# A four-layer graph network on one core: the flag load of SP moved ahead of its store waits, and sixteen identity transposes at the start of TensorE

## The reference

```python
h = jnp.maximum(_layernorm(x, axis=-1), 0.0)
x = x + _L0_gnn_ref(h, adj, L0_gnn_W, L0_gnn_a)     # GAT: Wh, e = leaky(s1 + s2), masked softmax, attention @ Wh
h = jnp.maximum(_layernorm(x, axis=-1), 0.0)
x = x + _L1_gnn_ref(h, adj, a0, a1, a2, a3)         # four edge kinds, scores (h*a_r) @ h.T picked by adj, softmax, @ h
h = jnp.maximum(_layernorm(x, axis=-1), 0.0)
x = x + _L2_gnn_ref(h, None, adj, weight, bias)     # RGCN: sum over kinds of mask @ h @ weight_r, + bias
h = jnp.maximum(_layernorm(x, axis=-1), 0.0)
x = x + _L3_gnn_ref(h, adj, L3_gnn_W, L3_gnn_a)     # GAT again, then elu
```

## Time and profile before

| what | value |
|---|---|
| median of three executions | 287.89 us (287.56 to 288.56) |
| the profiled execution's own time | 288.05 us |
| its span, first to last instruction | 285.8 us |
| instructions | 8113 |
| TensorE, VectorE, ScalarE, GpSimd busy | 96%, 88%, 89%, 82% |
| HBM traffic | 13.05 MB read, 4.19 MB written, 60 GB/s over the span |

### The profile page before, as it was taken

How to read it: one execution, slowest core, us unless ns; L and a number is a source line. 1 busy time by engine, 2 the same in 40 slices (tenths; PEclk the granted TensorE clock), 3 DMA queues, 4 the chain that set the end, 5 groups by cost and what they waited for, 6 DMA issues and landing times.

```text
span 285.8 us, 8113 instructions
## 1 busy us (share of the span) xinstructions
PE 274.3 (96%) x2252; PEld 257.9 (90%) x2252; DVE 251.9 (88%) x1217; ACT 255.0 (89%) x850; POOL 234.1 (82%) x376
## 2 busy tenths in 40 slices
PE   3999999999999999999999999999999999998991
PEld 2999998888889999999999999888889999998991
DVE  4889999988878887899999999998898888799985
ACT  5998988799998888999999999799999889796994
POOL 4998787777747999999999988887755899999722
PEclk9999999999999999999999999999999999999998
DMA  6946645400000000015333201000000000001213
GB/s 216 319 127 179 177 142 147 167 2 2 0 0 3 0 2 2 3 37 150 98 109 114 73 22 41 18 18 2 1 2 1 3 0 0 3 3 54 76 58 115
DMA packets 15414, 17.79 MB, mean 62 GB/s; under 512 B 2180, under 2 KB 11272, under 8 KB 15368
## 3 DMA queue, kind: packets, MB, share of 16 engines
q1 hardware_dynamic: 15220, 17.18, 19.9%
q10 hardware_dynamic: 148, 0.07, 0.1%
HBM read 13.05 MB, written 4.19 MB: 60 GB/s over the span
## 4 chain that ended last, share of the span: by engine, by line
PE 87%; DVE 8%; ACT 2%; issue 1%; POOL 0%; DVEq 0%; POOLq 0%
PE bank L1001 26%; PE bank L943 10%; PE bank L919 9%; PE bank L948 9%; PE bank L877 7%; PE bank L986 5%; PE bank L956 5%; PE bank L968 5%; PE bank L998 4%; PE bank L903 3%; PE bank L950 2%; DVE pT L699 2%; DVE expy L735 1%; PE bank L922 1%; DVE st L624 1%
## 5 line engine op out<-in xcount | busy, mean ns | idle before, releaser
L367 POOL TENSOR_TENSOR rs<-mv,minus_half 128x2 f32<-128x2 f32 x128 | 89.8, 702 | 35.5 <-DVE mv L635 35.0
L1001 PE MATMUL bank<-val,pT 128*128 128x129 f32 x512 | 74.6, 275 | 0.0
L1001 PEld LDWEIGHTS bank<-val,pT 128*128 128x128 f32 x512 | 67.3, 192 | 0.0
L384 POOL TENSOR_TENSOR h<-h,rs 128x256 f32<-128x256 f32 x93 | 58.2, 626 | 2.3
L699 DVE SCALAR_TENSOR_TENSOR pT<-bank,val,edgesT 128x256 f32<-128x256 f32 x128 | 55.0, 471 | 0.8 <-PE bank L956 0.7
L624 DVE BATCH_NORM_STATS2 st<-x 128x6 f32<-128x128 f32 x192 | 45.2, 276 | 0.0
L527 ACT ACTIVATE val<-bank,val 128x128 f32<-128x128 f32 x128 | 44.3, 437 | 0.1
L635 DVE BATCH_NORM_AGGREGATE mv<-st 128x2 f32<-128x9 f32 x256 | 33.5, 172 | 10.8 <-DVE st L624 1.0
L919 PE MATMUL bank<-w_gat,hT 128*128 128x131 f32 x256 | 40.3, 281 | 0.0
L376 POOL TENSOR_TENSOR h<-x,mv 128x256 f32<-128x256 f32 x64 | 40.1, 626 | 0.0
L877 PE MATMUL bank<-ident,h 128*128 128x128 f32 x192 | 38.0, 280 | 1.4 <-ACT hT L495 1.1
(11 more groups left out here) (87 smaller groups left out, 662.7 us busy)
## 6 DMA issues: line engine op xcount, KB each, us to landing
edges<-in_adj SPq DMA_DIRECT2D x32, 256.0 KB, 2.9
xin<-in_x SPq DMA_DIRECT2D x32, 128.0 KB, 2.6
out_x<-result SPq DMA_DIRECT2D x32, 128.0 KB, 1.7
w_rel<-in_L_gnn_weight SPq DMA_DIRECT2D x1, 256.0 KB, 2.8
w_gat<-in_L_gnn_W ACTq DMA_DIRECT2D x1, 64.0 KB
w_gat<-in_L_gnn_W SPq DMA_DIRECT2D x1, 64.0 KB
a_rel<-in_L_gnn_a SPq DMA_DIRECT2D x4, 0.5 KB, 3.0
bias<-in_L_gnn_bias SPq DMA_DIRECT2D x1, 64.0 KB, 3.3
```

What stands on the lines that cost most here:

```text
L367: pool.tensor_tensor(rs[:, n % WIDE], mv[:, n % WIDE, :, 1], minus_half[:, :], ALU.pow).then_inc(rs_ready, 1)
L384: pool.tensor_tensor(h[:, n % HS, :, 0:D], h[:, n % HS, :, 0:D], rs[:, n % WIDE, :].rearrange("p (t o) -> p t o", o=1).to_broadcast([P, T, ...
L1001: last = pe.matmul(bank_o(n)[:, t], pT[:, n % 4, u, t * P:(t + 1) * P], values[:, u], start=(u == 0 and layer == 1), stop=(u == T - 1), sk ...
```

## The change

SP's program waits for the flag and loads it right after the last store was issued. The eight waits for the stores stand in a function now, which is called first thing inside the general program and once more behind the branch. TensorE gets a function spin, which transposes the identity into bank 7 so many times: eight times ahead of put_wT, four times between put_wT and put_wa, four times behind put_wa. Nothing reads what these transposes write.

```diff
             pipeline([(load_x, SP_LAG, FIRST), (load_edges, SP_LAG, FIRST), (store, SP_LAG + 1, LAST)])
-            for k in range(SLOTS):
-                sp.wait_ge(stored[k], 16 * ROUNDS)
+            def all_stored():
+                for k in range(SLOTS):
+                    sp.wait_ge(stored[k], 16 * ROUNDS)
 
             sp.wait_ge(flag_ready, 1)
             with sp.If(sp.value_load(flag[0:1, 0:1], min_val=0, max_val=P) > 0):
+                all_stored()
                 sp.sem_inc(g_step, 1)
                 sp.sem_inc(g_stored, 16)
...
                 sp.wait_ge(g_stored, 16 * B + 16)
+            all_stored()
...
+            def spin(times):
+                for _ in range(times):
+                    pe.transpose(bank[7][:, 0:P], ident[:, :], ident[:, :])
+
+            spin(8)
             put_wT(0, ps_w)
+            spin(4)
             put_wa(0, ps_w)
+            spin(4)
```

## The result

Four executions of the changed kernel took 290.57 to 291.25 us, median 291.02, against 287.89 before. The ratio is 1.0105, with a 95% interval of 1.0091 to 1.0119: slower by 3.1 us. I had forecast 287.8, with a range of 286.9 to 288.6.

What follows compares the result with a forecast made beforehand. TensorE was taken as the bound, idle only near start and end, with ScalarE equally limiting the start. The profiled 288.05 us, +0.37 at the start and -0.45 at the end, gave 287.97; 0.16 lower on the median, 287.8, range 286.9 to 288.6.

Steps and rivals of the forecast that it cites:

- They write a bank that nothing uses yet, so they cost only TensorE's time and queue place.: Start: the sixteen identity transposes cost only TensorE time, 0.215 us each; first transpose of h 1.05 us late.
- tail: End: the execution's time less the time at which VectorE has written the flag; 4.46 us in the kernel before.
- Rival B: Start: TensorE's clock rises later, following the later real work; 288.3 if moved rigidly, up to 289.4; chance 0.12.
- The gain of 0.45 us at the end: End: SP loads the flag before its store waits, leaving VectorE's drain at 285.1 last; 0.45 us saved.
- 0.37 us late: Start: exponentials and L956 of graph 3 come later, 0.57 from ScalarE less 0.20 won back.
- the gate: Start: L956 of graph 3, near 16.1 us, claimed to be reached by TensorE and ScalarE within 0.1 us.
- The 0.57 of ScalarE: Start: ScalarE's mask moves from 8.61 to 9.18 us, 0.57 late, with ScalarE back to back from there.
- The 0.20 to be won back: Start: ScalarE's 0.25 us wait for TensorE's L903 transposes before 11.44 shrinks by 0.20 with a faster TensorE.
- The rise of the clock near 7.9 us: Start: if identity transposes count as work, TensorE reaches 2.4 GHz near 7.9 us instead of about 11.2.
- Rival A: Start: the transposes leave the clock where it was, rising at 11.2 us; 287.95 on the median; chance 0.20.
- ScalarE as the limit of the start: Start: ScalarE runs back to back from 8.61 us, so time saved on TensorE alone buys nothing.
- rival C: Start: TensorE alone decides when L956 of graph 3 starts, so 1.2 us counts in full; 286.2; chance 0.12.

Runs made afterwards that it cites:

- e9: Kernel before plus sixteen identity transposes in TensorE's general program, which doesn't run: 290.23 us, ratio 1.0071.
- e4: The change with 36 instruction records taken out of TensorE's general program, which doesn't run: 287.61 us, ratio 0.9986.
- e10: The change plus sixteen identity transposes at TensorE's idle end: 287.71 us, ratio 0.9975.
- e14: e9 plus sixteen identity transposes at TensorE's idle end: 287.68 us, ratio 0.9983 to the kernel before.
- e7: The change plus two identity transposes at TensorE's idle end: 291.09 us, ratio 1.0111 to the kernel before.
- e1: SP's part alone, the change without its spin calls: 287.93 us, ratio 1.0008 to the kernel before.
- e5: SP's part plus sixteen identity transposes at TensorE's idle end, none at the start: 287.06 us, ratio 0.9975 to the kernel before.
- e3: Kernel before plus sixteen identity transposes at TensorE's idle end, between the last layer and the flag's matmul: 287.45 us, ratio 0.9982.
- e6: Kernel before plus one identity transpose at the start and fifteen at TensorE's idle end: 287.50 us, ratio 0.9985.
- e13: SP's part alone, with 36 records taken out of TensorE's general program, which doesn't run: 287.17 us, ratio 0.9963 to the kernel before.
- e2: Kernel before plus the sixteen transposes at the start, SP as before: 290.82 us, ratio 1.0095.
- e16: e5 run again on another chip: 287.12 us, ratio 0.9957 to the kernel before.
- e12: e11 plus sixteen identity transposes at TensorE's idle end: 286.98 us, ratio 0.9960 to the kernel before.
- e8: e4 with its sixteen transposes at the start replaced by eight fp32 products of the identity: 287.99 us, ratio 0.9997 to the kernel before.
- e11: SP's part plus seven identity transposes at the start, five ahead of put_wT and two behind it: 290.39 us, ratio 1.0069 to the kernel before.

## Why the prediction was wrong, by its own steps

- **"They write a bank that nothing uses yet, so they cost only TensorE's time and queue place."** This step failed. They also lengthen the code: sixteen transposes are 32 records, less one wait, so the target of TensorE's jump over the general program lies 31 records farther on. The branch then takes 3.5 to 4.0 us instead of 0.36. For the profiled execution I had forecast a tail of 4.46-0.45 = 4.01 us, and it is 6.65: 2.6 of the 3.3 us between 287.97 and 291.25. The rest is the flag, 1.0 us later instead of 0.37. e9 shows the slow branch with no other difference, and e4, e10 and e14 show it undone. That the branch waits for code shows in queue 8: in all five kernels with a slow branch two blocks come behind its start, in the others one or none, and the branch is longer by as much as the first block takes longer. The Trainium skill, "Runtime: NRT & Kernel Launch", Instruction fetch mechanics, says so: a taken branch whose target isn't in the current window of two pages forces the target's page to be fetched before the engine goes on. The trace agrees, with a branch of 3.53 us here. I had not weighed it, and no rival of mine held it. Rival B's sign was right, its mechanism wasn't: the clock didn't rise later (between 9.8 and 12 us in the kernels with sixteen transposes, and at 7.6 in e7, against 10 to 12 without).
- **The gain of 0.45 us at the end.** VectorE's drain was the last, as forecast. SP drains 1.5 us behind the flag (e1, e5), not 1.1: the waits behind its jump cost 0.4 more, just what the forecast could bear. But alone the part is worth nothing that can be told (e1, ratio 1.0008). With work at TensorE's idle end the tail falls from 4.46 to 4.03 without SP's part (e3, e6 at 4.04, e14 at 4.02) and to 3.60 with it, and with shorter skipped code to 3.68 (e13). SP's 0.43 is there, but hidden behind a second end. I had read VectorE's drain as next in line, and not what lies outside the span: 2.25 us in the kernel before and 2.6 in e1, but 287.49-285.7 = 1.8 in e3 and 1.9 in e13. What ends there is open: the next block of TensorE's code comes behind the jump in e13 as it does in e1.
- **"0.37 us late"** at the gate. The direction was right and the size too small. Over five kernels with sixteen transposes (the change, e2, e4, e7, e10) the gate is at 16.77 on average, over the nine with none or one (before, e1, e3, e5, e6, e9, e13, e14, e16) at 16.11: 0.66. The 0.57 of ScalarE was nearly right (mask at 9.25 in e4, forecast 9.18). The 0.20 to be won back needed the early clock, which came in one of the five profiled executions. In the kernel's time it is less sure: 0.4 to 0.7 us, e10 against e12.
- **The rise of the clock near 7.9 us.** In e7 it came at 7.6, so identity transposes can raise the clock: TensorE had done little else until 6.8. Rival A, and with it what the Trainium skill says of transposes ("TensorE: Matmul & The Clock Gate", Part 4: PE-mode transpose), doesn't hold for that one execution if taken strictly. In the four others no rise came before 9.8, so it is no forecast either.
- **ScalarE as the limit of the start** held in the one execution that can test it: e7 shows TensorE waiting for it, and the gate moved by 0.18 us only. That speaks against rival C.

**Not settled:** what makes the block come near 280 us. Fifteen or sixteen transposes at the idle end did it in all six kernels that have them, two did not (e7). But e4 and e8 have the same count of records and differ there, so a count of records ahead of the jump doesn't explain it. Nor is it known what ends last outside the span in the kernel before and e1, or what the 2.3 to 2.4 us of a slow branch are that its block doesn't take.

One sum of the prediction is off by a hundredth: 287.89-0.6-0.45 is 286.84, not 286.85. It changes nothing.

## What to carry to other kernels

Code that never runs has a price where an engine jumps over it: look at the duration of every engine's branch and at the instruction fetches around it before and after adding instructions, however idle the engine is. Where the branch is slow, shorten what is jumped over, or give the engine work in its idle time ahead of the jump (sixteen transposes did it here, two did not), and test a candidate by lengthening the skipped code alone. This is shown for TensorE; in no run here was another engine's branch slow. A small gain at the end is real only if no other engine, and nothing outside the span, ends at the same time.

## What the runs showed that I had not expected

A difference of 13 records in a TensorE program of 5,000 made 2.5 us (e11 against e1). And nothing in the kernel before was placed with that in mind: the same sixteen transposes cost 2.8 us at the start (e2) and 2.1 us in skipped code (e9), and gain 0.5 us at the end (e3).
